# A four-part change to a two-layer hybrid megakernel: scores ahead of values in two attention streams, masks first, identity loaded alone, last tiles in their own banks

## The reference, cut to what matters

```python
scores = jnp.einsum('bhqd,bhkd->bhqk', q, k) / np.sqrt(KV_DIM)   # 16 heads, 256 x 256
scores = jnp.where(causal, scores, -jnp.inf)
attn = jax.nn.softmax(scores, axis=-1)
ctx = jnp.einsum('bhqk,bhkd->bhqd', attn, v)
...
h = jax.nn.gelu(jnp.einsum('lne,he->lnh', x, proj1) + proj1_bias, approximate=False)
out = jnp.einsum('lnh,eh->lne', h, proj2) + proj2_bias           # H = 1024
```

## Time and profile before

| what | value |
|---|---|
| timed runs, median (lowest, highest) | 1379.94 us (1372.92, 1380.36) |
| the profiled execution | 1378.08 us, span 1376.2 us |
| TensorE matmul busy | 1230.8 us (89%), 6928 instructions |
| VectorE busy | 743.3 us (54%) |
| ScalarE busy | 420.4 us (31%) |
| GpSimd busy | 79.7 us (6%) |
| mean granted TensorE clock | 0.97 |
| chain that ended last | TensorE 57%, VectorE 22%, issue 10%, ScalarE 8% |

### The profile page before, as it was taken

One profiled execution on the slowest core, in us unless ns is written; L12 is line 12 of the kernel. 1 busy time (PEld: TensorE's weight loads), 2 busy tenths in 40 slices (PEclk: granted clock), 3 DMA queues, 4 the chain that ended last, 5 costly groups with the idle time before them and its releaser, 6 DMA issues.

```text
span 1376.2 us, 17785 instructions
## 1 busy us (share of the span) xinstructions
PE 1230.8 (89%) x6928; PEld 932.1 (68%) x6928; DVE 743.3 (54%) x1712; ACT 420.4 (31%) x909; POOL 79.7 (6%) x69
## 2 busy tenths in 40 slices
PE   6889898999999999978788898989899999898887
PEld 5567475665876778767566764747668677787666
DVE  5553288696447447444634333877954564564451
ACT  3533020221332343433553420202223222423352
POOL 0000000000210120010000000000001101200000
PEclk9999999999999999999998999999999999999999
DMA  9100000000000000000000000000000000000000
GB/s 388 55 1 0 0 1 0 1 1 0 1 0 1 1 1 1 1 1 8 1 9 1 1 1 0 1 0 1 0 1 1 1 1 1 0 1 1 1 1 16
DMA packets 3410, 17.33 MB, mean 13 GB/s; under 512 B 256, under 2 KB 2304, under 8 KB 2816
## 3 DMA queue, kind: packets, MB, share of 16 engines
q1 hardware_dynamic: 2896, 14.12, 2.5%
q10 hardware_dynamic: 432, 2.08, 0.4%
HBM read 15.15 MB, written 1.05 MB: 12 GB/s over the span
## 4 chain that ended last, share of the span: by engine, by line
PE 57%; DVE 22%; issue 10%; ACT 8%; POOL 2%; DMA 0%; DVEq 0%; POOLq 0%; ACTq 0%
PE bank L652 52%; ACT scr L1244 3%; DVE scr L1737 3%; DVE scr L1736 2%; DVE scr L1754 2%; DVE scr L1753 2%; PE bank L669 2%; DVE XnT L1910 1%; DVE scr L1679 1%; DVE XnT L1912 1%; DVE scr L1514 1%; DVE stat L1506 1%; POOL rstd L2056 1%; ACT L1293 1%; DVE X L1499 1%
## 5 line engine op out<-in xcount | busy, mean ns | idle before, releaser
L652 PE MATMUL bank<-pack,scr 128*128 128x512 f32 (+2 forms) x944 | 312.7, 484 | 10.9 <-ACT scr L1222 8.9
L652 PE MATMUL bank<-XnT,pack 128*128 128x256 f32 x1024 | 260.5, 396 | 16.4 <-ACT XnT L1222 7.2
L652 PEld LDWEIGHTS bank<-pack,scr 128*128 128x128 f32 x944 | 178.4, 193 | 119.5 <-issue 94.7
L652 PE MATMUL bank<-scr,pack 128*128 128x256 f32 x944 | 236.1, 391 | 19.0 <-DVE scr L1679 18.1
L652 PEld LDWEIGHTS bank<-XnT,pack 128*128 128x128 f32 x1024 | 197.6, 197 | 52.4 <-ACT XnT L1222 9.6
L652 PEld LDWEIGHTS bank<-scr,pack 128*128 128x128 f32 x944 | 183.3, 196 | 51.3 <-DVE scr L1679 21.4
L1679 DVE TENSOR_TENSOR scr<-bank,scr 128x256 f32<-128x256 f32 x112 | 47.3, 424 | 118.3 <-ACT scr L1293 116.1
L1222 ACT ACTIVATE scr<-bank 128x512 f32<-128x512 f32 (+7 forms) x112 | 51.1, 473 | 192.5 <-PE bank L652 96.3
L1244 ACT ACTIVATE scr<-bank,negmax 128x256 f32<-128x256 f32 (+1 forms) x256 | 82.7, 444 | 88.9 <-DVE negmax L1596 88.8
L1293 ACT ACTIVATE scr<-bank 128x256 f32<-128x256 f32 x112 | 42.0, 383 | 216.4 <-PE bank L652 155.5
L1594 DVE TENSOR_REDUCE negmax<-bank 128x2 f32<-128x512 f32 x64 | 43.9, 685 | 79.8 <-PE bank L652 79.8
(11 more groups left out here) (177 smaller groups left out, 1436.1 us busy)
## 6 DMA issues: line engine op xcount, KB each, us to landing
pack<-pack_dram SPq DMA_DIRECT2D x1, 6152.0 KB, 18.5
pack<-pack_dram SPq DMA_DIRECT2D x1, 2180.0 KB, 29.9
pack<-pack_dram SPq DMA_DIRECT2D x1, 1595.0 KB, 24.0
X<-x SPq DMA_DIRECT2D x4, 256.0 KB, 19.0
pack<-pack_dram SPq DMA_DIRECT2D x1, 1024.0 KB, 20.6
out_dram<-X SPq DMA_DIRECT2D x4, 256.0 KB, 2.1
pack<-pack_dram ACTq DMA_DIRECT2D x1, 975.5 KB, 6.4
pack<-pack_dram SPq DMA_DIRECT2D x1, 793.5 KB, 25.4
```

The costliest lines, as they stand in the source:

```text
L652: return pe.matmul(o, l, r, start=start, stop=stop, skip_group_check=True)
```

## The change

Four things, in the code's words:
1. `stream(..., ahead=True)` for the first attention of sequences 0 and 1 and for the last attention of sequence 3. There a pass is scores i+1, values i-1, weights i, values_t i-1, the copy of `pv` is VectorE's, and no identity matmuls are issued.
2. In every `scores`, the mask matmul comes first in its bank, as soon as that bank is drained, and the score matmuls are added to it.
3. The identity's 128 columns of pack 0 are loaded by themselves; the rest of pack 0, the masks, pack 1 and x of sequence 1 wait until x of sequence 0 is there.
4. `ffn_half` waits for each piece of h where it is used. For the last FFN the two halves have banks of their own, and are added and stored one by one.

```diff
+        LAST = [(1, B - 1)]
...
             stream(stage, units(0, 0) + units(0, 1),
-                   {5: [("out_in", 0, 0)], 6: [("out_proj", 0, 0), ("norm_x", 1, 0)], 7: [("norm_t", 1, 0)]})
+                   {5: [("out_in", 0, 0)], 6: [("out_proj", 0, 0), ("norm_x", 1, 0)], 7: [("norm_t", 1, 0)]}, True)
...
-            stream(stage, units(1, d), {})
+            stream(stage, units(1, d), {}, True)
...
-        def stream(stage, todo, beside):
+        def stream(stage, todo, beside, ahead=False):
...
+                if ahead:
+                    if i + 1 < len(todo):
+                        unit("scores", i + 1)
+                    scores_first[0] = True
+                    if i:
+                        unit("values", i - 1)
+                    scores_first[0] = False
+                    if i < len(todo):
+                        unit("weights", i)
+                    if i:
+                        unit("values_t", i - 1)
+                    others(i)
+                    continue
                 if i:
                     alone[0] = not beside.get(i - 1)
                     unit("values", i - 1)
...
             for s in range(B):
+                if s == 1:
+                    sp.wait_ge(x_loaded[0], 16)
                 if s == S:
                     sp.wait_ge(loaded[1], 16)
                     for g in range(2, len(packs)):
                         sp.dma_start(pk[g][:, :], packs[g]).then_inc(loaded[g], 16)
                 sp.dma_start(X[s][:, :, :], x_in[s].rearrange("(a p) d -> p a d", p=P)).then_inc(x_loaded[s], 16)
-            for s in range(B):
+            for s in range(B - 1):
                 sp.wait_ge(x_final[s], 1)
                 sp.dma_start(out[s].rearrange("(a p) d -> p a d", p=P), X[s][:, :, :]).then_inc(x_stored, 16)
-            sp.wait_ge(x_stored, 16 * B)
+            for a in range(NT):
+                sp.wait_ge(x_final[B - 1], a + 1)
+                sp.dma_start(out[B - 1, a * P:(a + 1) * P, :], X[B - 1][:, a, :]).then_inc(x_stored, 16)
+            sp.wait_ge(x_stored, 16 * (B - 1 + NT))
...
             def latent(_, s):
                 wait_drained(pe, ("xnT", 0, s))
+                if s == 0:
+                    pe.wait_ge(loaded[0], 16)
...
                 for j in range(NB):
-                    claim(pe, ("sc", k, s, u, j))
+                    o = claim(pe, ("sc", k, s, u, j))[:, 0:HW].rearrange("p (c t) -> p c t", c=3)
+                    mm(o[:, 0::2, :], identb[:, :], negb[:, :].unsqueeze(1).broadcast_to([P, 2, P]), True, False)
                 for tile in (1, 0):
                     for j in range(NB):
                         o = bank[ring.bank(("sc", k, s, u, j))]
                         r0 = slice(32 * j, 32 * j + 32)
-                        mm(o[:, P:HW] if tile else o[:, 0:P], QT[s][r0, t, tile * P:(tile + 1) * P],
-                           KpT[s][r0, v, 0:(tile + 1) * P], tile == 1)
-                for j in range(NB):
-                    o = bank[ring.bank(("sc", k, s, u, j))][:, 0:HW].rearrange("p (c t) -> p c t", c=3)
-                    mm(o[:, 0::2, :], identb[:, :], negb[:, :].unsqueeze(1).broadcast_to([P, 2, P]), False)\
-                        .then_inc(full[ring.bank(("sc", k, s, u, j))], 1)
+                        last = mm(o[:, P:HW] if tile else o[:, 0:P], QT[s][r0, t, tile * P:(tile + 1) * P],
+                                  KpT[s][r0, v, 0:(tile + 1) * P], False)
+                        if tile == 0:
+                            last.then_inc(full[ring.bank(("sc", k, s, u, j))], 1)
...
-                if a == 0:
-                    for i in range(HT1 // 2):
-                        wait_drained(pe, ("h", r, i))
-                    claim(pe, ("fy", r))
-                o = bank[ring.bank(("fy", r))]
-                last = group(o[:, a * D:(a + 1) * D],
-                             [(HT[s][:, m, a * P:(a + 1) * P], w2[:, m, :]) for m in range(HT1)])
-                if a == NT - 1:
-                    last.then_inc(full[ring.bank(("fy", r))], 1)
+                if a == 0 or r in LAST:
+                    claim(pe, ("fy", r) + (a,) * (r in LAST))
+                key = ("fy", r) + (a,) * (r in LAST)
+                o = bank[ring.bank(key)]
+                for m in range(HT1):
+                    if a == 0 and m % 2 == 0:
+                        wait_drained(pe, ("h", r, m // 2))
+                    last = mm(o[:, a * D:(a + 1) * D], HT[s][:, m, a * P:(a + 1) * P], w2[:, m, :], m == 0, m == HT1 - 1)
+                if a == NT - 1 or r in LAST:
+                    last.then_inc(full[ring.bank(key)], 1)
...
-            pe.wait_ge(loaded[0], 16)
+            pe.wait_ge(ident_loaded, 16)
...
             def values(k, su):
                 s, u = su
+                if scores_first[0]:
+                    return
                 key = ("pv", k, s, u)
                 wait_full(act, key)
                 act.activation(pvs[s][:, u % PR, :], psum(key, T), ACT.Copy).then_inc(pvs_ready[s], 1)
...
-            act.dma_start(pk[0][:, :], packs[0]).then_inc(loaded[0], 16)
+            act.dma_start(pk[0][:, 0:P], packs[0][:, 0:P]).then_inc(ident_loaded, 16)
+            act.wait_ge(x_loaded[0], 16)
+            act.dma_start(pk[0][:, P:], packs[0][:, P:]).then_inc(loaded[0], 16)
             act.dma_start(pk[1][:, :], packs[1]).then_inc(loaded[1], 16)
             act.dma_start(raw, masks).then_inc(masks_loaded, 16)
...
+            def values(k, su):
+                s, u = su
+                if not scores_first[0]:
+                    return
+                key = ("pv", k, s, u)
+                wait_full(dve, key)
+                dve.tensor_copy(pvs[s][:, u % PR, :], psum(key, T)).then_inc(pvs_ready[s], 1)
...
             def ffn_out(k, s):
+                if (k, s) in LAST:
+                    settle()
+                    for a in range(NT):
+                        key = ("fy", (k, s), a)
+                        wait_full(dve, key)
+                        dve.tensor_tensor(X[s][:, a, :], psum(key, NT * D)[:, a * D:(a + 1) * D], X[s][:, a, :],
+                                          ALU.add).then_inc(drain_of(key), 1)
+                        wait_drained(dve, key)
+                        dve.sem_inc(x_final[s], 1)
+                    return
                 key = ("fy", (k, s))
                 residual(key, s)
                 if k == 1:
                     dve.sem_inc(x_final[s], 1)
 
             def consts(_, s):
-                dve.wait_ge(loaded[0], 16)
+                dve.wait_ge(ident_loaded, 16)
```

More of the change, by code:

```diff
@@ L279, in hybrid_kernel @@
         masks_loaded = sem("masks_loaded")
+        ident_loaded = sem("ident_loaded")
         trig_in, trig_out = sem("trig_in"), sem("trig_out")
@@ L402, in pv_pairs @@
                     bV[s][:, a].unsqueeze(1).broadcast_to([P, n, HD, NH]))
-        halves, weave, summing, alone = [False], [False], [False], [False]
+        halves, weave, summing, alone, scores_first = [False], [False], [False], [False], [False]
         def lanes(name, k, s):
@@ L2034, in _ @@
             table = dict(spread2=spread2, delta_sq=delta_sq, consts=consts, top_exp=nothing, ffn_half=nothing, delta_expand=delta_expand, delta_diag=delta_diag, conv_tap=conv_tap, gates=gates, down_sum=nothing, angles=angles, norm_x=norm_x, norm_t=nothing, latent=latent, kv=kv, kv_fold=kv_fold,
-                         scores=scores, weights=weights, values=nothing, values_t=values_t, out_in=nothing, out_proj=out_proj, router=router, spread_t=nothing, spread=spread, x_first=x_first,
+                         scores=scores, weights=weights, values=values, values_t=values_t, out_in=nothing, out_proj=out_proj, router=router, spread_t=nothing, spread=spread, x_first=x_first,
                          x_second=x_second, down=down, lora_t=lora_t, lora=lora,
```

## The result

The changed kernel takes 1359.03 us (median of 4 runs, 1355.22 to 1359.39) against 1376.43 (1372.35 to 1380.36) for the kernel before on the same chip: ratio 0.9852, 95% interval 0.9833 to 0.9872. The profiled executions, 1378.08 before and 1358.74 after, lie 19.3 apart, their spans 19.6. The forecast was 1364, from a sum of 14.7 of gain.

What follows compares the result with a forecast made beforehand. TensorE, busy 89% of the span, was taken as the bound, so edits pay only where it waits. Terms -7.6 - 4.4 - 1.7 - 1.0 = -14.7 from 1378.1 gave 1363.4, stated as 1364; 8-in-10 range 1357 to 1371.

Steps and rivals of the forecast that it cites:

- The two streams: First attention (sequences 0 and 1) and last (sequence 3): shorter passes gain 7.6 us and 4.4 us.
- The ring: One pass of these streams: exponentials, banks free, scores, maxima, exponentials; 5.11 us (bounds 4.9 and 5.5) against 6.53.
- The end: Last FFN: later h waits, a 256-column last residual and a store half as large gain 1.7 us.
- The start: Loads: X of sequence 0 lands earlier with only the identity beside it; gain 1.0 us, bounds -2.1 and +1.4.
- Rival D: Start: X of sequence 1 lands last, +1.4 instead of -1.0, 1365.8 us; inside the forecast's 0.60.
- the loss of 0.5: Start: about 2 us fixed cost per DMA would delay the second load group, so the part ends near +0.5.
- The middle: Between the first and last streams: no net change, 0; over 4 us of change would make the prediction wrong.
- rival C: Middle: half-speed clock stretches fall elsewhere as start times move; 1371 or 1357 us, chance 0.09 each side.
- theory M: Raised after the measurement: masks in front gain the middle's 4.9 us in the streams there.
- masks in front of the other streams: Streams outside the two: same matmuls, 0.1 lost or 0.3 won where a first maximum is waited for; taken as 0.
- Rival A: The two streams: passes shrink half as much, to 5.8 us, giving 1368.6 us; chance 0.18.
- B: The two streams: without filler TensorE's clock falls to half and the kernel ends slower, 1393 us; chance 0.04.

Runs made afterwards that it cites:

- d1: The changed kernel with the values copy of the two streams back on ScalarE; 1367.87 us in one profiled execution.
- c2: The kernel before, unchanged, executed and profiled once more; 1382.47 us.
- b1: The changed kernel with the mask matmuls behind the scores again; ratio 0.9879 to the kernel before.
- c1: The changed kernel with 36 identity matmuls on TensorE ahead of the first router matmuls; ratio 0.991 to the kernel before.
- a1: The kernel before with only the new order of the two streams (scores first, values copy on VectorE, no identity matmuls); ratio 0.9898.
- f1: The changed kernel with identity matmuls in six idle times of the middle and more filler in shorter ones; mean 1352.4 us, ratio 0.9808 to the kernel before.
- a3: The kernel before with only the new loads: identity by itself, the others behind x of sequence 0; ratio 0.9982.
- a2: The kernel before with only the mask matmuls in front of the scores; ratio 0.9997.
- a4: The kernel before with only ffn_half's later waits and the last FFN's two banks and stores; ratio 0.9985.
- c0: The changed kernel run again without further change; ratio 0.9863 to the kernel before, mean 1361.1 us.
- h1: The changed kernel with 12 matmuls of zeros on TensorE from about 1 us, ahead of its first transposes; ratio 0.9883 to the kernel before.
- k2: The kernel before with 2 identity matmuls ahead of the router of token step 1 of sequence 2; 1378.95 us in one profiled execution.

## Why the prediction was right or wrong

**The two streams: right.** The ring was read from the right rows, and 5.11 came out as 4.99 to 5.09. From the exponentials of unit 0 to those of unit 7 it took 33.84 against a forecast of 33.8; that this is so near is partly luck, since unit 2 came 8.0 behind unit 0 and not 7.6, and the shorter passes made up for it. -7.6 became -8.2 since the tail took 10.65 instead of 11.1, and the 0.1 for the masks didn't show. -4.4 was -4.3. The remark that VectorE's 4.0 us fit was right; that the copy "stood behind nothing" on ScalarE was true of the tail alone, and d1 shows what it would have cost in the ring.

**The end: right, 0.6 too small.** -1.7 was -2.3, and seven of nine profiles with that code have 27.77 to 27.83 (the other two a clock below 1.00 there). From the context transposes to ffn_half it was 1.44 shorter (1.27 forecast), the residual gave the 0.27, and from its end to the span's end 2.62 became 2.20: 0.4 for the store that I put at 0.2.

**The start: right on average, wrong in the pair.** -1.0 was 0.0 between the two profiles. Nine profiles with the old loads have E0 at 27.74 to 29.28, mean 28.61; eight with the new ones and no zeros in front 26.48 to 28.10, mean 27.59. That is the forecast's -1.0, but partly by luck: TensorE's first transposes start 1.4 earlier in the mean (7.04 against 8.44), and 0.4 of it is lost behind them. Much of the spread is the low clock of TensorE's first matmuls, for which the forecast had no term: the twelve take 4.32 to 5.49, by the execution. The profile of before happened on 4.72 and on the earliest start, 8.00. Rival D (X of sequence 1 late) didn't occur: it was used at 8.24 instead of 9.69. So the loss of 0.5 that the prediction estimated from 2 us of fixed cost a transfer did not come. (The section of the Trainium skill that it cites there, "Anatomy of one DMA" in "DMA: Bandwidth & Descriptors", tells of transfers that GpSimd issues; these are SyncE's and ScalarE's.)

**The middle: the step that failed.** I took it as 0, and gave 0.18 to rival C, that the half-speed stretches fall elsewhere, 7 us either way. It was -4.9, over the 4 us that I had named as making me wrong, with 10.2 us less at half speed. That the half-speed stretches fall elsewhere is what happened, and C's size was in range. C's reason, that all start times move, is not what the runs show in the main: c2 and b1 kept the pattern of before at other start times; for it speak c1, and a1, whose pattern differs from b1's though both have the new streams and no masks in front. The edit that goes with the new pattern is masks in front. Two of its steps, +4.7 between the norms at 649 and 727 and -4.5 behind them, came in every profile with masks in front (the first smaller in c1 and both in f1) and nearly cancel. The third, -4.8 between 1127.6 and 1217.9, came in all nine of them, and stands where the instructions are the same in both kernels. So theory M had the right edit and the wrong way: the masks show no saving of their own in the middle, and what changes with them is where the clock falls. The clearest pair are a3 and a2, which run the same instructions 0.14 us apart:

```profile
1160.06 3.68 PE L655 MATMUL bank<-XnT,pack 128*128 128x256 f32 x8
```

```profile
1159.92 1.99 PE L652 MATMUL bank<-XnT,pack 128*128 128x256 f32 x8
```

The first is a3's, the second a2's. My error was to treat the clock's part as a rival beside a forecast with a sharp zero. It has no zero: an edit of the order ahead can draw a new pattern for the 1240 us behind (masks in front did, a3's loads and a4's end did not, behind the norm at 240), and a term of 0 with some 5 us either way, inside the forecast, would have said that.

The other term that I put at nothing was masks in front of the other streams, weighed as 0.1 lost against 0.3 won. The runs show a loss: 0.24 a pass in the old order, 0.5 between the norms at 535 and 600, 3.1 for a2 as a whole at equal clock. Only in the new order do they win, 0.17 a pass (b1).

**The sum.** Direct terms, averaged as far as the profiles allow: -8.2 - 4.3 - 2.3 - 1.0 = -15.8, against -14.7. The runs show 18.9 (c0) and 20.4 (first runs) by their ratios, with intervals of about 4 and 2.7 either way. Of the 3 to 5 left over, the first lies within its interval, and they are not all the clock's. A line fitted to 49 runs of the kernel before and 10 of the changed one, time against half-speed time (from each run's mean granted clock), gives 0.32 us for each us at half speed and 17.1 between the kernels at equal clock, 1.0 either way; their plain means are 19.6 apart. So the clock's part was about 2.5 us in the runs, where the pair of profiles had 4.9 in the middle, and 1.3 over the direct terms stays unexplained. On c0's chip the mean clocks were almost the same (0.9692 and 0.9687), and the means 18.7 apart. Part may be in 74.8 to 94.2: five of nine profiles with the old streams lost 3.0 to 4.6 there, of seven with the new ones (without c1's filler and d1) only two did. Not settled is whether that share is lasting, since the timed runs have no windows.

Rival A fell by the pass, and B by the clock of 1.00 in both streams: the idle pieces of up to 1.9 us and the missing filler did not bring it down in the pair. h1 and f1 show that this was not sure. With other start times the same stream had 0.74 and 0.83 from 60 to 80. What B said of the clock can happen, at a price of 3 to 5 us up to the norm at 94 and not of 18.

## What to carry to other kernels

An edit that changes the order or spacing of the work ahead can also draw anew where the clock falls: compare stretch by stretch at fixed marks, with the granted clock beside each, before a difference is given to code, and compare timed runs at equal mean clock. a2 looked like no change, and was by that measure a loss of 3 us under a better clock. Fill TensorE's 4 us idle times first; here 82 identity matmuls gave 17.8 us, as much as the whole change. More is not always better: f1 filled shorter ones too and was 9 slower. When a copy is moved off the critical engine, look at what stands behind its reader in order, not at the engine's busy sum.

## What the runs showed of the hardware

- The same half-speed pattern came back for over a thousand us in two executions of one program whose start times differ by 4.5 us (before and c2), and in b1 9 us earlier, and a move of 0.2 to 0.4 us (k2) changed it.
- The middle's length went with its time at half speed: in the 15 profiles without filled idle times from 61.4 us at half speed and 1230.4 us (c1) to 93.0 and 1242.6 (a3), by a straight line 0.38 us for each us at half speed, no profile more than 2.6 us off it.
- Mean granted clock and time go together from run to run: in the 11 runs of the kernel before beside c0, 1372.64 at 0.974, 1378 to 1381 at 0.968 to 0.970, 1382.2 to 1383.0 at 0.966, about 1.2 us for each 0.001 there, and 0.9 by the line through 59 runs of both kernels.
- After its first matmuls at 7.0 to 8.8 us TensorE stayed at the low clock until the twelve projection matmuls were partly or wholly done (4.32 to 5.49 instead of 2.86). Twelve 512-column matmuls of zeros from 0.99 on were enough to have it up by 8.34.
